# The message stage of a graph network: four factors per edge read from PSUM, unread products left out

## The reference

```python
s, v = node_feats[:, :32] @ W_up_s, einsum('nui,uw->nwi', node_feats[:, 32:].reshape(n, 32, 3), W_up_v)
tpw = silu(silu(edge_feats @ A1 + b1) @ A2 + b2) @ A3          # 128 weights of an edge: w0 w1 w2 w3
ss, vs = s[sender], v[sender]
y_s, y_v = edge_attrs[:, :1], edge_attrs[:, 1:4]               # the edge's numbers
out_s0 = ss * y_s * w0
out_s3 = einsum('eui,ei->eu', vs, y_v) / sqrt(3) * w3
out_v1 = ss[:, :, None] * y_v[:, None, :] * w1[:, :, None]
out_v2 = vs * y_s[:, :, None] * w2[:, :, None]
message = segment_sum(concat([out_s0, out_s3, out_v1, out_v2]), receiver)   # then a linear map of each node
```

## Time and profile before

| | us |
|---|---|
| median of 3 runs | 3237.64 (3234.07 to 3239.08) |
| the profiled execution, its own time | 3245.87 |
| its span | 3244.2 |
| message stage, first gather issued to last scan's end | 2441.55 to 2965.53 |
| PE busy in the span | 2492.4 (77%) |
| DVE busy | 2008.5 (62%) |
| ACT busy | 1440.9 (44%) |
| POOL busy | 2017.4 (62%) |

### The profile page before, as it was taken

One profiled execution on the slowest core, in us unless ns is written; L12 is line 12 of the kernel. 1 busy time (PEld: TensorE's weight loads), 2 busy tenths in 40 slices (PEclk: granted clock), 3 DMA queues, 4 the chain that ended last, 5 costly groups with the idle time before them and its releaser, 6 DMA issues. The chain is left out here.

```text
span 3244.2 us, 52779 instructions
## 1 busy us (share of the span) xinstructions
PE 2492.4 (77%) x14692; PEld 1922.0 (59%) x14692; DVE 2008.5 (62%) x4643; ACT 1440.9 (44%) x3085; POOL 2017.4 (62%) x1928
## 2 busy tenths in 40 slices
PE   1679994777776677997677777374787999996887
PEld 1456664777775345665577777333674666664676
DVE  6764444777775475443677777344436888886444
ACT  0134443555553563443455555254443555553444
POOL 5467886777777657886777777655106777775000
PEclk9975556899898886555899899686888999997898
DMA  9869997778886657999687877565636666663653
GB/s 291 227 202 375 381 388 215 227 226 230 224 229 153 157 137 278 390 357 339 183 232 222 230 224 225 131 92 185 171 110 172 192 191 195 193 194 100 244 192 121
DMA packets 557663, 715.66 MB, mean 221 GB/s; under 512 B 126898, under 2 KB 441849, under 8 KB 531557
## 3 DMA queue, kind: packets, MB, share of 16 engines
q1 hardware_dynamic: 210932, 424.05, 38.4%
q0 software_dynamic: 107392, 156.15, 20.9%
q10 hardware_dynamic: 239104, 132.59, 14.0%
HBM read 331.57 MB, written 381.07 MB: 220 GB/s over the span
## 5 line engine op out<-in xcount | busy, mean ns | idle before, releaser
L1792 POOL DMA_INDIRECT att_rows<-table,kvrow x784 | 743.5, 948 | 274.0 <-issue 233.7
L1819 PE MATMUL att_pq<-wide,att_near 128*128 x1568 | 358.3, 314 | 274.9 <-DVE att_prod L2010 125.6
L2427 POOL DMA_INDIRECT msg_rows<-rows,msg_src x392 | 384.4, 981 | 261.6 <-DMA msg_src<-in_src_pt 142.4
L1562 POOL DMA_INDIRECT matrix<-count,place x294 | 459.5, 1563 | 89.5 <-issue 88.8
L1632 DVE COPY tab_part<-tab_bank 128x512 f32<-128x512 f32 x400 | 257.3, 686 | 322.0 <-DMA table<-tab_part 270.5
L1819 PEld LDWEIGHTS att_pq<-wide,att_near 128*128 128x128 f32 x1568 | 265.0, 212 | 307.3 <-issue 304.8
L1673 PE MATMUL tab_bank<-wk,tab_kv 32*128 32x256 f32 x1600 | 363.0, 694 | 33.1 <-DVE tab_part L1632 24.2
L1657 ACT ACTIVATE tab_part<-tab_bank 128x512 f32<-128x512 f32 x400 | 221.6, 594 | 320.5 <-DMA table<-tab_part 291.5
L1821 PE MATMUL att_pq<-wide,att_far 128*128 x1568 | 336.3, 300 | 0.0
L1673 PE MATMUL tab_bank<-wv,tab_kv 32*128 32x256 f32 x1600 | 331.4, 617 | 0.0
L1673 PEld LDWEIGHTS tab_bank<-wk,tab_kv 32*128 32x128 f32 x1600 | 203.8, 301 | 183.3 <-DVE tab_part L1632 154.8
(11 more groups left out here) (475 smaller groups left out, 5484.4 us busy)
## 6 DMA issues: line engine op xcount, KB each, us to landing
table<-tab_part SPq DMA_DIRECT2D x200, 1024.0 KB
att_sums<-att_out ACTq DMA_DIRECT2D x196, 272.0 KB
gcn_cells<-matrix SPq DMA_DIRECT2D x50, 808.0 KB
att_message<-in_ea_rows SPq DMA_DIRECT2D x98, 256.0 KB
sums<-att_out ACTq DMA_DIRECT2D x98, 256.0 KB
msg_hidden<-hidden SPq DMA_DIRECT2D x196, 128.0 KB
sums<-msg_out ACTq DMA_DIRECT2D x98, 256.0 KB
nb_cells<-matrix SPq DMA_DIRECT2D x25, 808.0 KB
```

The source lines that it names most:

```text
L1562: nc.gpsimd.indirect_dma_start(D.matrix, place, K.count[:, col:col + 1], None, compute_op=ALU.add).then_inc(added[b % BLOCKS], 16)
L1792: nc.gpsimd.indirect_dma_start(rows[g % RR][:, j, :], None, D.table, bass.IndirectOffsetOnAxis(ap=K.kvrow[:, t:t + 1], axis=0)).then_inc(r ...
L1819: nc.tensor.matmul(pq[g % 2][:, j * P:(j + 1) * P], near[g % RE][:, j, :], queries[:, bass.ds(window[j], 1), :].rearrange("p t d -> p (t d ...
L2427: nc.gpsimd.indirect_dma_start(rows[g % RR][:, j, :], None, D.rows, bass.IndirectOffsetOnAxis(ap=src[:, t:t + 1], axis=0)).then_inc(rows_i ...
```

## The change

The matmuls into `idle` go, and with them the bank. A bank `factors` takes its place: two halves, each for eight groups of 4 x 4 numbers in each partition. Every eighth group DVE first copies numbers 1 to 4 of the next eight groups' edges from `edge` into one half (the last time of the two groups that are left) and counts that in a new semaphore, `laid`; from the third span on it waits beforehand until the row products that read that half have been done. The row product waits for `laid` and takes its second operand from `factors`, in PSUM, instead of from `edge`, in SBUF. Nothing else differs.

```diff
-        idle = s.ps("idle")
+        laid, SPAN = s.sem("laid"), 8
+        factors = s.ps("factors")[:, 0:2 * SPAN * J * 4].rearrange("p (u g j c) -> p u g j c", u=2, g=SPAN, j=J)
...
             for g in range(G):
-                for j in range(J):
-                    nc.tensor.matmul(idle[:, j * P:(j + 1) * P], K.ident[:, :], K.all_ones[:, :], start=True, stop=True)
...
                 if g >= 2:
                     dve.wait_ge(turned, 2 * (g - 1))
+                u, n = g // SPAN % 2, min(SPAN, G - g)
+                if g % SPAN == 0:
+                    if g >= 2 * SPAN:
+                        dve.wait_ge(scaled, g - SPAN)
+                    nc.vector.tensor_copy(factors[:, u, 0:n, :, :], edge[:, g:g + n, :, 1:5]).then_inc(laid, 1)
+                dve.wait_ge(laid, g // SPAN + 1)
                 nc.vector.tensor_tensor(sc[g % 2][1][:, :, :].rearrange("p j (b c) -> p j b c", c=32),
                                         rows[g % RR][:, :, :].rearrange("p j (b c) -> p j b c", c=32),
-                                        edge[:, g, :, 1:5].unsqueeze(3).broadcast_to([P, J, 4, 32]), ALU.mult).then_inc(scaled, 1)
+                                        factors[:, u, g % SPAN, :, :].unsqueeze(3).broadcast_to([P, J, 4, 32]), ALU.mult).then_inc(scaled, 1)
```

## The result

The changed kernel took 3253.39 us (median of 5 runs, 3237.01 to 3264.48) against 3237.64: ratio 1.0052, 95% interval 1.0031 to 1.0073. It is slower by 16 us, half a per cent; 22 were forecast. Its runs spread over 27 us, the five of before over 7. In the longer series of the experiments the kernel before spreads over 14 to 18 us (17 to 32 runs), so five runs say little of a spread.

The account below looks back on a forecast made before the run. PE paced the message stage at 5.13 us a group; without that, POOL's 4.99 plus 0.42 held by the scan gives 5.41: loads +26, tail -4, together +22 us, 3260 from the median 3237.64; range 3247 to 3273.

Parts of the forecast that it names:

- PE and the unread products: Message stage: without the unread products' 0.89 us, PE needs 4.24 us a group instead of 5.13 and no longer paces.
- The scan holds the loads, not the row product: Message stage, steady state: the scan, reading two SBUF operands, makes one POOL load a group 0.14 us too long.
- The sum: POOL's loads: hold chance 0.82 times mean 0.51 is 0.42 us a group; period 4.99 + 0.42 = 5.41, +26 us.
- The tail: Message stage's end: last row product up to 2.1 us earlier, unread products' 1.8 us gone; -4 us.
- From the profiled execution to the median: Whole program: +22 us makes 3268 by the profiled execution, 3260 from the runs' median of 3237.64.
- What strews the holds: Message stage: landing jitter of 1 us against load spacing of 1.25 puts the scan's held window anywhere over the loads.
- DVE's pace: DVE in the message stage: able to do 4.35 us a group, it catches up and then waits for landed rows.
- The check by phases: Scan against loads two groups later: periods of 5.0 or 5.62 us, mean 5.31, +12 us.
- Rival A: Message stage: loads run free with steady landings, period 4.99 to 5.05; 3219, or up to 3226; chance 0.28.
- Rival B: Message stage: DVE, waiting for PE, still trails and locks; period 5.11 to 5.20, 3231 to 3240 us; chance 0.11.
- Rival C: PE in the message stage: its clock falls once it idles, 7.2 us a group, +200 us, 3440; chance 0.03.
- Only the load is held: DVE and POOL in the message stage: in a collision only the load is held, and only that is priced.

## Why the prediction was right

The forecast was 22 us slower, the result is 16, inside the range, on the forecast's side.

- *PE and the unread products.* Their 0.89 us went, PE stands idle in each group, and PE no longer sets the pace. Taken away alone they cost as much as the whole change; put back they cancel it (1.0010).
- *The scan holds the loads, not the row product.* Right, and tested from both sides: with the scan's sum in PSUM 0 of 89 loads under it are held; with the row product's factors in PSUM 0 of 37. The forecast took for granted that an operation with one operand in PSUM holds no load. The trace of the kernel before agrees: of its 276 loads that start under a gradient product, a weight product or a sum (at least 0.13 before its end), each with one operand in PSUM, none takes more than 0.953 us.
- *The sum.* Chance of a hold 0.82, measured 80 of 98; mean 0.51, measured 0.49; so 0.40 us a group for 0.42, and the period 5.40 for 5.41. In the profiled execution this is 97 x 0.26 = 25 us for 26. That it fits to 0.01 is luck in part. The sum takes the loads' starts as spread evenly against the scan. Here they nearly are; without the products alone none fell between 0.4 and 0.6 us behind a scan's start, and the scan held 67 with 0.36 on average (period 5.30), though the same sum gives at least 5.41 there.
- *The tail* was mis-sized: from the end of the last load (2966.1) to the last scan's end (2984.1) it is 17.9 us, before it was 20.4. It gave 2.5 us back and not 4. The last row product did start earlier, by 3.3 us for the 2.1 of the sum (3.60 us after the last load, before 6.94). But from there to the last scan's end it took 14.3 us where it had taken 13.5; the 1.8 us that the unread products were to free on this way did not show. PE waits there 2.82 us for ACT's copy before it turns the last rows, at 2971.73.
- *From the profiled execution to the median.* I carried the gain of one execution over to the median. The stage's 22.8 us in the profiled one are those of the slowest of five runs; the median is 16. One profile is one draw. Whether the other runs had shorter holds, or a shorter rest of the program, which varies as much, no run here shows; so where the 6 us between 22 and 16 went stays open.
- *What strews the holds.* I put it down to the landings, whose jitter of 1 us was to place the scan's window anywhere over the loads. With short landings, steady for stretches, the long holds stayed and the period was 5.50. So the forecast's path holds (DVE catches up, the holds grow), but this cause of the spread isn't shown. Nor did "nearly all landings lie between 4.6 and 5.0" hold in the kernel before: two in three do.
- *DVE's pace.* I had it at 4.35 us with only the rows to wait for. It also waits 43.5 us for ACT's copies of the turned rows; it still stays under the loads' period, so it cost nothing, but by it the scan stands 3.3 to 3.65 us behind the row product, not 3.13 (the starts that I read add up to 3.16).
- *The check by phases* was wrong as a forecast of a fixed value: with short landings it gave 5.05 and 5.50 was measured. The statistical sum, which it was to check, held for this kernel.
- *Rival A* failed since the scan's hold remained; its condition (nothing holds) gives its period, 4.994, once it is made. *Rival B* failed: DVE did wait for rows. But its lock at a pace near 5.1 is what the kernels with an unread pace show. *Rival C* failed: granted clock 1.00 in the stretch above, 0.97 over the whole stage (0.98 before).
- *Only the load is held.* I priced no hold of DVE by a load that already runs, and the trace shows none: in the kernel before 90 scans start 0.1 to 0.7 us into a running load, and all take 1.273 to 1.276 us.
- *Slips of the text.* The 784 products are records of the profile, two for each of 392 matmuls. A hold of 0.55 a group gives 3272 and not 3274. Neither moves the forecast.

## What to carry to other kernels

Before taking filler work off an engine that looks like the bound, ask what it keeps in step: here PE's useless 0.89 us held DVE behind the gathers, where each collision cost 0.14 us and not 0.49. When gathers are issued by POOL, look at what DVE runs at the start of each longer one, and move to PSUM an operand of the operation that does the holding, which need not be the one that the change has in mind. Here, with the unread products gone, the sum's move to PSUM took the held time from 30.3 us (24.2 under the scan, 6.1 under the row product) to 7.2. A steady state that repeats exactly can't tell two suspects apart; the stage's first few groups can.

## What the runs showed of the hardware that I had not expected

- This program was slowed by giving an engine less to do, sharply: PE at 5.04 us a group, total 3223; at 4.91, total 3241; at 5.13, total 3232.
- The unread product with 112 moving columns took its 0.11 us a pass all the same (0.88 for eight); with 112 stationary columns too it took 0.78 for eight. The weight load's own record is 0.192 us at the median in the first case, as with 128, and 0.178 in the second. So here the distance changed when the stationary columns did and not with the moving columns alone; what sets it, no run shows.
- In the changed kernel the scans that start 0.04 to 0.09 us ahead of a load took 1.296 to 1.342 us for a median of 1.274, and the loads, 0.943 to 0.952, weren't held. With the sums in PSUM no scan took more than 1.281. The row product did either, in the run with only its two operands in SBUF: one that starts 0.024 ahead took 0.747 and its load 0.947, one that starts 0.022 ahead took 0.664 and its load was held (the pair shown at 2639.94). In the kernel before neither was slowed when it started 0.1 to 0.7 us into a load: 90 scans took 1.273 to 1.276, and 92 row products 0.664 to 0.693, within the 0.658 to 0.693 of all.
- The twelve copies of 128x128 float32 from SBUF into PSUM took 0.29 us on average, like their opposite; the 0.283 in the line above has the smaller last one in it.
